# A four-layer graph and attention network on one core: the order of the two groups' products in the loops of the linear attentions

## The reference, cut to what matters

```python
q, k, v = (elu(q) + 1, elu(k) + 1, v)              # q, k, v = (normed x) @ W + bias, per head
kv    = einsum('hnd,hne->hde', k, v)               # the key-value sums
k_sum = k.sum(axis=nodes)
z     = 1 / (einsum('hnd,hd->hn', q, k_sum) + eps)
out   = einsum('hnd,hde->hne', q, kv) * z
x     = x + out @ W_proj + b
```

## Time and profile before

| | us |
|---|---|
| median of 3 runs | 3196.98 (3196.13 to 3199.22) |
| profiled execution: its time | 3200.5 |
| profiled execution: its span | 3198.7 |
| PE busy in the span | 3013.3 (94%) |
| DVE busy | 1826.3 (57%) |
| POOL busy | 1457.2 (46%) |
| ACT busy | 739.2 (23%) |

### The profile page before, as it was taken

The page is one execution under the profiler, slowest core; times in us unless marked ns, Lnnn a source line. Parts: engine busy times, 40 slices in busy tenths (PEclk is TensorE's granted clock), DMA queues, the critical chain, the costliest instruction groups (busy, mean ns, idle before and its releaser), DMA issues.

```text
span 3198.7 us, 38315 instructions
## 1 busy us (share of the span) xinstructions
PE 3013.3 (94%) x13757; PEld 2339.4 (73%) x13767; DVE 1826.3 (57%) x2916; ACT 739.2 (23%) x1287; POOL 1457.2 (46%) x1007
## 2 busy tenths in 40 slices
PE   8999989999999998898999989899999998999988
PEld 3467567878888886576878458578888886878855
DVE  7834589665555566657786746644444447743342
ACT  1043221233322312201226221211111112212122
POOL 2022368534444553464433044466666664545620
PEclk9999999899999998999999999999999999999999
DMA  2011347311122232232221142123333332222313
GB/s 84 16 45 45 99 144 232 100 58 60 60 69 65 74 97 81 66 125 68 69 60 30 60 129 60 59 80 96 92 90 97 98 98 69 78 66 74 98 41 138
DMA packets 93011, 261.69 MB, mean 82 GB/s; under 512 B 10535, under 2 KB 11175, under 8 KB 92596
## 3 DMA queue, kind: packets, MB, share of 16 engines
q1 hardware_dynamic: 79488, 217.09, 22.3%
q10 hardware_dynamic: 13396, 42.91, 4.0%
HBM read 258.39 MB, written 1.57 MB: 81 GB/s over the span
## 4 chain that ended last, share of the span: by engine, by line
PE 83%; DVE 11%; issue 3%; ACT 2%; DMA 0%; ACTq 0%; DVEq 0%
PE ps L444 22%; PE ps L448 22%; PE ps L449 22%; PE ps L955 3%; DVE aux L2254 3%; PE ps L563 1%; PE ps L847 1%; PE ps L836 1%; PE ps L829 1%; PE ps L821 1%; DVE hot L2729 1%; DVE row L2053 1%; PE ps L557 1%; PE ps L633 1%; PE ps L1042 1%
## 5 line engine op out<-in xcount | busy, mean ns | idle before, releaser
L379 POOL TENSOR_SCALAR w_hi<-raw 128x768 fp32r<-128x768 f32 x498 | 486.7, 977 | 1565.3 <-PE ps L444 1397.4
L382 POOL TENSOR_TENSOR w_lo<-raw,w_hi 128x768 fp32r<-128x768 f32 x498 | 979.2, 1966 | 41.5
L444 PE MATMUL ps<-A_hi,w_hi 128*128 128x512 f32 x924 | 364.5, 395 | 2.2 <-DVE sel_now L2548 1.5
L448 PE MATMUL ps<-A_lo,w_hi 128*128 128x512 f32 x924 | 360.7, 390 | 0.0
L449 PE MATMUL ps<-A_hi,w_lo 128*128 128x512 f32 x924 | 360.0, 390 | 0.0
L444 PE MATMUL ps<-H_hi,w_hi 128*128 128x512 f32 x804 | 319.3, 397 | 21.1 <-issue 11.6
L449 PE MATMUL ps<-H_hi,w_lo 128*128 128x512 f32 x804 | 316.3, 393 | 0.0
L448 PE MATMUL ps<-H_lo,w_hi 128*128 128x512 f32 x804 | 316.2, 393 | 0.0
L444 PE MATMUL ps<-B_hi,w_hi 128*128 128x512 f32 x576 | 234.7, 407 | 14.9 <-issue 7.5
L449 PE MATMUL ps<-B_hi,w_lo 128*128 128x512 f32 x576 | 226.3, 393 | 0.0
L448 PE MATMUL ps<-B_lo,w_hi 128*128 128x512 f32 x576 | 226.2, 393 | 0.0
(11 more groups left out here) (537 smaller groups left out, 5740.1 us busy)
## 6 DMA issues: line engine op xcount, KB each, us to landing
raw<-stream_dram SPq DMA_DIRECT2D x552, 384.0 KB, 3.0
w_ring<-w_dram ACTq DMA_DIRECT2D x51, 384.0 KB, 3.6
u_rows<-rows_dram ACTq DMA_DIRECT2D x8, 768.0 KB, 6.2
rows<-rows_dram ACTq DMA_DIRECT2D x7, 768.0 KB, 4.3
w_last<-w_dram ACTq DMA_DIRECT2D x9, 384.0 KB, 3.6
x<-x_dram ACTq DMA_DIRECT2D x1, 1536.0 KB, 9.3
head_f<-w_dram ACTq DMA_DIRECT2D x4, 384.0 KB, 6.1
out_dram<-x ACTq DMA_DIRECT2D x1, 1536.0 KB, 5.1
```

What stands on the lines that cost most here:

```text
L379: pool.tensor_scalar(w_hi[:, b // 3, b % 3], raw[:, b // 3, b % 3], 1.0, 1.0, ALU.mult, ALU.mult)\
L382: pool.tensor_tensor(w_lo[:, b // 3, b % 3], raw[:, b // 3, b % 3], w_hi[:, b // 3, b % 3], ALU.subtract)\
L444: mm = pe.matmul(o, wh, xh, start=first, stop=False, skip_group_check=True)
L448: pe.matmul(o, wh, xl, start=False, stop=False, skip_group_check=True)
```

## The change

The matmuls and the DVE instructions are the same in kind and number. On the PE the key-value sums of group 0 stand ahead of the queries of group 1, and the outputs of group 0 ahead of the sums of group 1. On the DVE the copies of the sums of group 0 stand ahead of q_t of group 1. The first wait of the DVE for outputs is folded into its wait for the sums of group 1 (three tiles at once, in the PE's order). ACT's program stays as it is.

```diff
--- before.py
+++ after.py
@@ -748,6 +748,21 @@
 
             def linear_attention(X, what):
 
+                def keys_values(g):
+                    pe.wait_ge(dve_to_pe, S.due(dve_to_pe))
+                    use(6 + g)
+                    for m in range(NT):
+                        mm = pe.matmul(ps[:, 6 + g, 0:P + 2], k_n[:, g, m], v_n[:, g, m], start=m == 0, stop=m == NT - 1,
+                                       skip_group_check=True)
+                    done(mm, 6 + g, "dve")
+
+                def outputs(g):
+                    pe.wait_ge(bank_free["dve"][6 + g], S.coming(bank_free["dve"][6 + g]))
+                    use(3 * g)
+                    done(pe.matmul(ps[:, 3 * g], kv[:, g], q_t[:, g], start=True, stop=True), 3 * g, "dve")
+                    use(3 * g + 1)
+                    done(pe.matmul(ps[:, 3 * g + 1], k_sum[:, g], q_t[:, g], start=True, stop=True), 3 * g + 1, "dve")
+
                 with S.loop(what, 3) as i:
                     for g in range(2):
                         blocks(2)
@@ -765,22 +780,14 @@
                             if m % 2 == 1:
                                 done(mm, b, "dve")
                         blocks_used(2, False)
+                        if g == 1:
+                            keys_values(0)
                         blocks()
                         tile_t(3 * g, g, 2, X, "act")
                         blocks_used()
-                    for g in range(2):
-                        pe.wait_ge(dve_to_pe, S.due(dve_to_pe))
-                        use(6 + g)
-                        for m in range(NT):
-                            mm = pe.matmul(ps[:, 6 + g, 0:P + 2], k_n[:, g, m], v_n[:, g, m], start=m == 0, stop=m == NT - 1,
-                                           skip_group_check=True)
-                        done(mm, 6 + g, "dve")
-                    for g in range(2):
-                        pe.wait_ge(bank_free["dve"][6 + g], S.coming(bank_free["dve"][6 + g]))
-                        use(3 * g)
-                        done(pe.matmul(ps[:, 3 * g], kv[:, g], q_t[:, g], start=True, stop=True), 3 * g, "dve")
-                        use(3 * g + 1)
-                        done(pe.matmul(ps[:, 3 * g + 1], k_sum[:, g], q_t[:, g], start=True, stop=True), 3 * g + 1, "dve")
+                    outputs(0)
+                    keys_values(1)
+                    outputs(1)
                     S.due(dve_to_pe, 2)
                 n = S.seen[dve_to_pe.name]
                 return [n - 4] * 4 + [n - 1, n]
@@ -2492,6 +2499,13 @@
                 S.step(dve.memset(same[HD:P, HD:P], 1.0))
                 S.step(dve.memset(v_n[:, :, :, P:P + 2], 1.0))
                 dve.wait_ge(rows_in, S.due(rows_in, 16))
+
+                def keys_values(g, tiles):
+                    dve.wait_ge(tile_for["dve"], S.due(tile_for["dve"], tiles))
+                    dve.tensor_copy(kv[0:HD, g, 0:HD], ps[0:HD, 6 + g, 0:HD])
+                    dve.tensor_copy(kv[HD:P, g, HD:P], ps[HD:P, 6 + g, HD:P])
+                    freed(dve.tensor_scalar(k_sum[:, g], same[:, :], ps[:, 6 + g, P:P + 1], None, ALU.mult), 6 + g)
+
                 with S.loop(what, 3) as i:
                     for g in range(2):
                         c = bass.ds(i * 256 + g * P, P)
@@ -2511,16 +2525,15 @@
                                 out=k_n[:, g, 2 * half:2 * half + 2].rearrange("p m c -> p (m c)"),
                                 in0=scr[:, 2 + half, 0:256], scalar=1.0, in1=scr[:, 2 + half, 256:512], op0=ALU.min,
                                 op1=ALU.add)
+                        if g == 1:
+                            keys_values(0, 1)
                         dve.wait_ge(act_to_dve, S.due(act_to_dve))
                         dve.scalar_tensor_tensor(out=q_t[:, g], in0=scr[:, 0], scalar=1.0, in1=scr[:, 1], op0=ALU.min,
                                                  op1=ALU.add).then_inc(dve_to_pe, 1)
+                    keys_values(1, 3)
                     for g in range(2):
-                        dve.wait_ge(tile_for["dve"], S.due(tile_for["dve"]))
-                        dve.tensor_copy(kv[0:HD, g, 0:HD], ps[0:HD, 6 + g, 0:HD])
-                        dve.tensor_copy(kv[HD:P, g, HD:P], ps[HD:P, 6 + g, HD:P])
-                        freed(dve.tensor_scalar(k_sum[:, g], same[:, :], ps[:, 6 + g, P:P + 1], None, ALU.mult), 6 + g)
-                    for g in range(2):
-                        dve.wait_ge(tile_for["dve"], S.due(tile_for["dve"], 2))
+                        if g == 1:
+                            dve.wait_ge(tile_for["dve"], S.due(tile_for["dve"], 2))
                         freed(dve.tensor_scalar(row[:, :], ps[:, 3 * g + 1], eps, None, ALU.add), 3 * g + 1)
                         S.step(dve.reciprocal(row[:, :], row[:, :]))
                         freed(dve.tensor_tensor(aux[:, 2 + g], ps[:, 3 * g], row[:, :], ALU.mult), 3 * g)
```

## The result

The changed kernel takes **3210.53 us** (median of 6 executions, 3208.38 to 3216.09) against 3197.28 for the one before: 13.25 us more, ratio 1.0044 (95% interval 1.0034 to 1.0054; the ratios are estimated from all executions, so they differ a little from those of the medians). The forecast was 3204.4 (3200 to 3210): the sign was right, the size about half. The profiled execution took 3215.33 us.

What follows compares the result with a forecast made beforehand. The PE was taken as the bound (83% of the chain), waiting 1.47 us for q_t nine times. Loops 5.8 us (7 x 0.71 plus 2 x 0.42) plus clock 1.6 gave 7.4 over 3196.98: 3204.4 us, range 3200 to 3210.

Steps and rivals of the forecast that it cites:

- The shift of the query tile: On the PE, group 1's query tile begins 0.95 us later, behind the sums of group 0.
- POOL and the DVE holding each other: POOL's splits and the DVE's k_n, k_sum and q_t stretch each other; q_t ends 0.77 us later than before.
- The waits: At each iteration's end the PE waits 0.74 us for q_t and 1.65 us for k_sum, in place of 1.64.
- 0.71 us an iteration and 0.42 at the two other ends: Loss at seven iteration ends, 0.71 us each, and behind the second and third attention, 0.42 each: 5.8 us.
- The clock: The granted PE clock falls about once at the ends of iterations, costing 1.6 us; extremes 0 and 14.4 us.
- The rest of the loop is PE work and shifts with it: Behind the new waits, the remaining loop work on the PE only moves later, by 0.71 us per iteration.
- Rival A: The clock falls at most iterations; nine falls cost 14.4 us, giving 3217; chance 0.12 in part or whole.
- nine falls: Upper extreme of the clock term: a fall at every iteration's end, 14.4 us.
- B: Rival: POOL doesn't hold group 1's k_sum on the DVE; loss 1.8 us, 3198.8, not slower; chance 0.14.
- C: Rival: the shortened wait for q_t wins, up to 0.9 us an iteration, 3189; chance 0.04.
- The same waits are in every execution: Ground for adding the sum of 7.4 us to the median of 3196.98 us, not to the profiled execution's 3200.5.

Runs made afterwards that it cites:

- e6: Changed kernel with k_sum made by a tensor_tensor (one input in PSUM) in place of a tensor_scalar: 3200.89 us, ratio 1.0008 to the kernel before.
- e3: Changed kernel with six extra matmuls, never read, between the sums and the outputs of group 1: 3205.25 us, ratio 1.0024 to the kernel before.
- e7: The changed kernel again, nothing altered, for a third profile: 3204.45 us.
- e10: Kernel before, order untouched, with ten unread matmuls of ones between the first attention's loop and its gat_logits: 3198.19 us.
- e11: Kernel before, order untouched, with twenty unread matmuls of ones between the first attention's loop and its gat_logits: 3206.84 us.
- e9: Kernel before, PE order untouched, with k_n's own signal; DVE order copies of group 0, q_t, copies of group 1: 3199.13 us, ratio 1.0003.
- e4: Changed kernel with k_n's own signal; sums of group 1 right behind the query tile, ahead of outputs of group 0: 3189.69 us, ratio 0.9973 to before.
- e1: Changed kernel with the outputs of group 0 put back behind the sums of group 1: 3208.26 us, ratio 1.0029 to the kernel before.
- e2: Changed kernel with the sums of group 0 put back behind the query tile, only outputs moved ahead: 3197.27 us, ratio 0.9996 to before.
- e12: The kernel of e2 again, for a second profile: 3199.48 us.

## Why the prediction was right in its sign and wrong in its size

- *The shift of the query tile, 0.95 us*: measured 0.90.
- *POOL and the DVE holding each other*: I had k_sum of group 0 end at the split's end plus 0.08, the second splits at 0.84 and 1.81, q_t 0.55 behind a w_lo, k_sum of group 1 0.08 behind one. Measured: 0.83 and 1.81, 0.55, 0.08. e6 takes the hold away and the time with it.
- *The waits, 0.74 and 1.65 us from start to start*: measured 0.66 and 1.67.
- *0.71 us an iteration and 0.42 at the two other ends, 5.8 us*: measured 0.75 and 0.41, 6.1 us. The behaviour of the loops was right.
- *The step that failed is "The clock", 1.6 us for about one fall*. It measured 4.8 us for three falls at ends of iterations, in two of three profiles of the changed kernel; e3, which fills the new wait, has none and is 5 us faster than the change. The third profile (e7) has no excess at all over the loops, so the term needed a range from 0 to 5 us. TensorE: Matmul & The Clock Gate of the Trainium skill (Why this matters for your kernels) warns of a long idle gap between bursts of matmuls. Here waits of 0.5 and 1.5 us with a us of work between sufficed at three ends of nine, so the trace shows that shorter ones can do it too.
- *"The rest of the loop is PE work and shifts with it"* held in the loops, but I took it for all that follows. In the graph part the PE and the DVE race, and who waits depends on the clock. That is 2.7 us, in no term of the sum and in no rival, the second step that failed. e10 and e11 show that a mere delay does such a thing, and e7 that the changed kernel can come without it. With 3.2 us more for the clock, 2.7 here and 0.3 in the loops the forecast's 7.4 us become 13.6, against 13.25 measured.
- *Rival A* was the nearest: 5.8 + 4.8 lies between the forecast and its nine falls. I gave it and the upper end too little. B is near what e6 makes of the kernel (3200.9 us against B's 3198.8). C is out: nothing came sooner. *The same waits are in every execution* was true, but the clock isn't, and the kernel before alone ranged from 3188 to 3204 us.

## What to carry to other kernels

Ask from which event the chain hangs that the engine waits for, here the end of the query tile. Work that doesn't need that event is worth most behind it, as cover; moved ahead of it, it lengthens the loop by nearly its own length (0.75 us for 0.90 of matmuls here). That is only as good as the chain's length is known: e9 keeps all such work behind the event, e4 has a part of it ahead, and e4 was the faster by 0.93 us an iteration. And ask whether a wait is for what the instruction really needs: the sums waited for q_t, and k_n was there 3.1 us earlier (1545.97 against 1549.11 in the earlier trace rows).

A term for the clock needs its own range where PE waits are added, even short ones, and a small change is judged by stretches of the trace with the same clock, not by the total alone.

## What the runs showed of the hardware

- The clock fell at the same three of nine ends in two profiles of the changed kernel. Falls at the ends that PE work follows at once came in the profiles of the two kernels with the most waiting there, 2.0 us (the changed one) and 2.4 us (e1), and in none with less: 1.9 us (e2), 1.5 (before), 1.4 (e6). Why some such ends bring a fall and others not isn't shown. Stops of 2.83 us behind the second attention brought a fall in the first profile of the changed kernel, against none in e12 with a stop of the same length:

```profile
2037.71 0.47 PE L444 MATMUL ps<-H_hi,w_hi 128*128 128x512 f32 x1 [2.83 <-issue]
...
2040.33 0.63 PE L448 MATMUL ps<-H_lo,w_hi 128*128 128x512 f32 x1
```

- The code ahead of the attentions is the same in all these kernels, and the end of the first query tile came between 1536.0 and 1546.2 us (kernels without the early sums). What makes the difference isn't shown: the granted clock over the first 1500 us was 0.97 or 0.98 in all of them.
- A tensor_scalar on 128 x 128 fp32 elements in SBUF took 0.86 us beside POOL's tensor_tensor, and up to 1.40, against 0.29 at the least (e4); a tensor_tensor with one input in PSUM took 0.29 beside it.
